# Grouped attention: spread and values issued ahead of the second pass of scores

## The reference

```python
q = rope((h @ Wq).reshape(B, S, 32, 128), pos)         # 32 query heads
k = rope((h @ Wk).reshape(B, S, 4, 128), pos)          # 4 key heads, 8 query heads each
v = (h @ Wv).reshape(B, S, 4, 128)
scores = einsum('bqhd,bkhd->bhqk', q, repeat(k)) / sqrt(128)   # causal mask
attn = softmax(scores, axis=-1)
o = einsum('bhqk,bkhd->bqhd', attn, repeat(v)).reshape(B, S, 32 * 128) @ Wo
x = resid + o
```

## Time and profile before

| | |
|---|---|
| time, median of 3 runs | 1534.93 us (1533.66 to 1537.94) |
| the profiled execution's own time | 1537.94 us |
| its span, first to last instruction | 1536.2 us |
| granted TensorE clock, mean of the span | 0.937 of full speed |
| busy in the whole span | PE 1342.8, DVE 961.9, ACT 792.4, POOL 617.7 us |
| the 64 steps of grouped attention | from about 750 to 1200 us |

### The profile page before, as it was taken

One profiled execution on the slowest core, in us unless ns is written; L12 is line 12 of the kernel. 1 busy time (PEld: TensorE's weight loads), 2 busy tenths in 40 slices (PEclk: granted clock), 3 DMA queues, 4 the chain that ended last, 5 costly groups with the idle time before them and its releaser, 6 DMA issues. The chain is left out here.

```text
span 1536.2 us, 23871 instructions
## 1 busy us (share of the span) xinstructions
PE 1342.8 (87%) x8621; PEld 987.4 (64%) x8621; DVE 961.9 (63%) x1625; ACT 792.4 (52%) x1590; POOL 617.7 (40%) x550
## 2 busy tenths in 40 slices
PE   5788678899799579886789999999999869999998
PEld 4564455644388434433557777776777658888887
DVE  4763754558755587873677777877787554333443
ACT  2455104345532246664567777777877544445442
POOL 5110001101054511211566666666676445555553
PEclk8999779989999678996899999999999979999999
DMA  2000400020000100002000000000000023233231
GB/s 70 1 1 2 121 3 0 4 101 0 1 1 1 38 1 2 2 2 81 7 14 15 15 25 19 15 22 22 15 22 8 8 87 121 96 119 110 105 119 51
DMA packets 29492, 55.58 MB, mean 36 GB/s; under 512 B 6506, under 2 KB 16170, under 8 KB 29204
## 3 DMA queue, kind: packets, MB, share of 16 engines
q1 hardware_dynamic: 29396, 54.30, 11.0%
HBM read 52.98 MB, written 1.21 MB: 35 GB/s over the span
## 5 line engine op out<-in xcount | busy, mean ns | idle before, releaser
L2606 DVE TENSOR_TENSOR e_act<-e_gated,ps 128x512 f32<-128x512 f32 x66 | 45.4, 688 | 158.1 <-POOL e_gated L2411 158.1
L1839 POOL TENSOR_TENSOR a_raw<-a_prod 128x512 f32<-128x512 f32 x72 | 98.3, 1366 | 51.7 <-DVE a_prod L2243 51.7
L1844 POOL TENSOR_TENSOR a_q_low<-a_raw,a_q_high 128x512 fp32r<-128x512 f32 x64 | 82.8, 1294 | 87.2 <-ACT a_q_high L2103 87.2
L2240 DVE TENSOR_TENSOR a_prod<-ps,a_rot 128x512 f32<-128x512 f32 x72 | 49.7, 691 | 93.9 <-PE ps L1888 93.7
L2411 POOL TENSOR_TENSOR e_gated<-e_gate,e_wb 128x512 f32<-128x512 f32 x66 | 85.2, 1292 | 49.8 <-ACT e_gate L2532 44.5
L1848 POOL TENSOR_TENSOR a_o_low<-a_o,a_o_high 128x512 fp32r<-128x512 f32 x64 | 82.9, 1295 | 41.7 <-ACT a_o_high L2154 39.7
L2111 ACT ACTIVATE a_shift<-ident,a_nmax 128x128 bf16<-128x128 f32 x256 | 81.9, 390 | 32.3 <-DVE a_nmax L2252 32.0
L2402 POOL TENSOR_TENSOR e_we_low<-e_we,e_we_high 128x768 fp32r<-128x768 f32 x33 | 60.8, 1842 | 89.5 <-ACT e_we_high L2537 85.5
L1606 DVE SCALAR_TENSOR_TENSOR m_acc<-ps,m_conv_w,m_acc 128x1020 f32<-128x1020 f32 (+2 forms) x60 | 76.0, 1275 | 31.3 <-ACT m_acc L1526 29.9
L1360 PE MATMUL ps<-m_ln_T,m_win 128*128 128x512 f32 x192 | 88.8, 618 | 4.2 <-DMA m_win<-in_m_winT 3.5
L601 DVE TENSOR_REDUCE x_nmax<-ps 128x2 bf16<-128x512 f32 x128 | 82.5, 689 | 11.2 <-PE ps L371 10.9
(11 more groups left out here) (431 smaller groups left out, 4271.2 us busy)
## 6 DMA issues: line engine op xcount, KB each, us to landing
e_wb<-token_weights SPq DMA_DIRECT2D x32, 512.0 KB, 3.9
e_we<-in_experts SPq DMA_DIRECT2D x33, 384.0 KB, 3.1
a_wq<-in_a_wq SPq DMA_DIRECT2D x16, 256.0 KB, 2.7
a_wo<-in_a_wo SPq DMA_DIRECT2D x16, 256.0 KB, 2.8
m_win<-in_m_winT SPq DMA_DIRECT2D x2, 1024.0 KB, 8.8
nf_pickU<-in_nf_pickU SPq DMA_DIRECT2D x2, 768.0 KB
nf_raw<-in_ffn_w SPq DMA_DIRECT2D x3, 352.0 KB
x<-in_x SPq DMA_DIRECT2D x4, 256.0 KB, 6.6
```

The lines of the kernel that those rows point to most:

```text
L1839: e.tensor_tensor(raw[:, i % 2, :], prod[:, i % 2, 0, :], prod[:, i % 2, 1, :], ALU.add).then_inc(s_raw, 1)
L1844: e.tensor_tensor(low_part, raw[:, i % 2, :], high_part.bitcast(F32), ALU.subtract).then_inc(s_xl, 1)
```

## The change

In TensorE's loop of the grouped attention, spread and values of step n - 4 are issued between the first scores of step n and the second scores of step n - 1, where they came behind both. Nothing else differs.

```diff
                 if n < N:
                     first_scores(n)
-                if 0 <= n - 1 < N:
-                    scores(n - 1)
                 if 0 <= n - PV < N:
                     spread(n - PV)
                     values(n - PV)
+                if 0 <= n - 1 < N:
+                    scores(n - 1)
                 for i in [*of_step.get(n, ())][:1]:
                     piece(i)
                 if 0 <= n - PO < N:
```

## The result

The changed kernel takes 1586.87 us (median of 4 runs, 1585.38 to 1593.71) against 1536.43 us before (4 runs): a ratio of 1.0341, 95% interval 1.0308 to 1.0374. The direction was forecast, the size was not: 1570.5 us with a range up to 1583. The two profiled executions stand 47.4 us apart (spans 1536.2 and 1583.6).

The account below looks back on a forecast made before the run. TensorE was taken to bound the stage, busy 392.14 of 405.00 us. Pairs behind keys 6.5, usual even steps 24.5, long splits 4.2 and step 4's 0.4 sum to 35.6 us; on 1534.93 that gives 1570.5 us, range 1560 to 1583.

Parts of the forecast that it names:

- The even steps: Usual pairs: values still wait for VectorE's division, then second scores follow; 1.36 us each in 18 steps, 24.5 us.
- Odd steps: Division ends 0.1 us before values could start, and ScalarE's exponentials keep 0.7 us of cover; cost 0.
- Pairs behind keys: Six pairs behind a piece of keys: 1.41 us less 0.33 from a 0.48 us split; 1.08 each, 6.5 us.
- The long splits: VectorE's split of inverses, 1.60 us instead of 0.48: 1.12 us per lost start; share kept, three steps, 4.2 us.
- the trace agrees: VectorE's split against GpSimd's sum: issue order decides who waits, and the edit leaves the order of these starts unchanged.
- The ends of the loop: First and last steps, where TensorE already waits for exponentials: 0.4 us for step 4, 0 from step 60 on.
- Steps 61 to 66 have gaps of their own: 0: Last steps of the loop: existing gaps were to absorb the moved scores, at no cost.
- The terms for step 4 and 60: Existing waits for exponentials absorb delay: step 4 costs 1.41 less 0.86, rounded down to 0.4 us; step 60 costs 0.
- (d): Rival: waits lower TensorE's granted clock, a tenth of the stage's columns at half clock, 39 us, 1610 us; 2%.
- (a): Rival: TensorE gets past the waiting spread and does the scores meanwhile; cost 0, 1535 us; 2%.
- (b): Rival: earlier values release division, low part and projection, closing TensorE's 12.86 us of gaps; at best 1522 us; 2%.
- (e): Rival: the chain is less tight than read, so half the price appears, 1553 us; 5%.

Follow-up runs that it names:

- spread_ahead: Kernel before with only spread moved ahead of the second scores, values left behind them; 1572.86 us, ratio 1.0267.
- values_ahead: Kernel before with only values moved ahead of the second scores, spread left behind them; 1589.31 us, ratio 1.0336.
- ordered_odd: Kernel before with the new order in odd steps only, and GpSimd waiting in even steps for VectorE's split; 1530.98 us, ratio 0.9967.
- odd_only: Kernel before with the new order in odd steps only, even steps in the old order; 1554.89 us, ratio 1.0137.
- ordered_new: Changed kernel, with GpSimd waiting in even steps for VectorE's split before its sum; 1577.98 us, ratio 1.0250 to the kernel before.
- filler_new: Changed kernel with 12 matmuls of a projection's form added in each of steps 4, 5 and 6; 1572.85 us, ratio 1.0289 to the kernel before.
- ordered_piece_old: Kernel before, old order, with the step's first piece right behind first scores and GpSimd waiting for the split; 1519.30 us, ratio 0.9900.
- ordered_old: Kernel before, old order, with GpSimd waiting in even steps for VectorE's split before its sum; 1523.70 us, ratio 0.9923.
- even_only: Kernel before with the new order in even steps only, odd steps in the old order; 1584.58 us, ratio 1.0339.

## Why the prediction was right in kind and wrong in size

- **The even steps.** Right, mechanism and size. Plain pairs grew by 1.43 us, 1.36 forecast; most of the difference is the second scores, which take 1.51 us behind values instead of 1.41 behind first scores. The 25 even steps from 10 to 58 were forecast at 32.75 us and came to 33.9 (396.89 - 362.99 between the sums of step 9 and 59). That three plain splits would be long again was luck: they are those of steps 14, 18 and 54, where they were 18, 32 and 46. spread_ahead and values_ahead have the pair lengths of the same chain to within 0.2 us, and with the piece early the price is gone from these steps.
- **Odd steps.** Right in plain pairs: the exponentials kept their place, and plain pairs of ordered_odd take 13.5 to 13.6. Behind a piece of keys the order in the odd step alone costs 0.66 us a pair (14.93 over 14.27), since TensorE waits 1.2 us for the division there.
- **Pairs behind keys.** 1.07 for 1.08 (15.30 to 16.37). The prediction's 0.48 us for these splits came true because the order of the two starts changed: before, GpSimd's sum starts 0.02 to 0.04 us ahead of the split, after, 0.04 to 0.05 behind it. That contradicts its own sentence that nothing in the edit changes that order. Against a kernel without long splits the price is 2.1 (14.27 to 16.37).
- **The long splits.** Step 4's is no toss: GpSimd starts within 0.02 us of it and it is long in both kernels. Of the tosses 3 of 22 were lost before, 4 of 28 after, 17 of 28 in odd_only, with the same 0.04 to 0.05 us between the starts; the unit price (1.1 us) was right, the odds are not steady. They do have a part in the profiled loss: step 60's split became a long one (1.1), and the low clock behind steps 4 and 60, 1.6 us each, is not in ordered_new, which has short splits there. That is up to 4.3 of the 46.0 us; that the long splits brought the low clock about is argued. The prediction's "the trace agrees" on the order of issue is too strong: at 878.06 VectorE starts first and its split is the one that lasts long.
- **The ends of the loop: the step that failed.** The prediction put "Steps 61 to 66 have gaps of their own: 0", step 60 at 0 and step 4 at 0.4, and priced step 6 as a plain one. Steps 4 to 6 cost 6.6 us for 1.8 (7.65 with the pair behind, for 2.84), step 60 and later 4.5 for 0. Of 46.0 us of loop that is 9.3 of the 10.4 that the sum of 35.6 lacks. The terms for step 4 and 60 would have held with short splits (0.48 and 0.32 in ordered_new); those for steps 5, 6, 62 and 64 would not. What stood there instead: the low clock three times, 1.6 us each by the blocks behind it (values and scores of step 4 last 4.26 us, 776.30 to 780.56, for 2.7 elsewhere), 4.8 together; steps 5 and 6 with waits 1.2 and 1.4 us longer than in plain steps (1.19 for none, 2.21 for 0.79), as no projection runs while VectorE rotates, which leaves 1.5 us over forecast and low clock; steps 62 and 64 with 1.4 us (0.6 and 0.8 in ordered_new too), where the split waits for ScalarE and the division ended 1.0 us ahead of values in the kernel before, less than the 1.41 us of scores that moved; a long split in step 60, 1.1. These make 8.8 of the 9.3.
- **The clock.** The rival (d) had 2% and was priced for the whole stage; what came was three short falls, 4.8 us. filler_new shows for steps 5 and 6 shorter waits and no fall, though its own 1.6 us can't be told from that of the waits there. What decides whether the clock falls stays open. The length of the wait in front of it alone does not: the waits for long splits at 862, 893 and 1179 us, 1.9 us each, and the 2.22 us at 801 left the granted clock at 1.00, the 1.90 at 1225 did not.
- **The other rivals.** (a) did not come: TensorE stood for the split in all 26 even steps with scores behind spread that needed nothing from it. In the Trainium skill ("TensorE: Matmul & The Clock Gate") the rule on the order of matmuls that the prediction cites stands under The mechanism, just ahead of the section that it names; these waits agree with it. (b), a gain, and (e), half the price, did not come either.
- **The rest** of the median, 50.4 us against 47.4 between the profiles, is scatter of executions: the kernel before ran from 1525.77 to 1543.87 us over all comparisons. Within a kernel the time mostly goes with the mean granted clock of the span, about 1 us for 0.001: the kernel before took 1525.77 us at 0.946 and 1538.00 at 0.935 in the last comparison, ordered_piece_old, with no long split in its trace, 1512.52 at 0.943 and 1523.96 at 0.933. That the number of long splits makes most of the scatter is not borne out: ordered_new, without any in its trace, ranges over 12.1 us.

## What to carry to other kernels

Before a block is moved ahead of another, look at what releases it: here an end 0.05 to 0.1 us ahead of its start, in all even steps up to 60, said that the block in front of it was the cover, and the whole block became the price. Price the first and the last turns of a pipelined loop one by one: a block that covers a wait in the middle (here the projection) may be missing there. And where the lengths of two engines' instructions depend on which of them gets going first, within a tenth of a microsecond, order them by a semaphore before anything is compared: an added wait made this kernel 0.8% faster.

## What was not expected of the hardware

- The split (two SBUF inputs, 128x256) takes 0.48 us and GpSimd's sum then 1.58, or 1.60 and 1.27. In both cases shown VectorE starts 0.05 us ahead. The Trainium skill ("SBUF — State Buffer", Who interferes with whom) says that issue order decides who blocks. The lengths agree nearly: the pair takes 1.63 or 1.60 us, the two alone 0.48 + 1.28 = 1.76. The starts agree in part. In all kernels without GpSimd's wait the split was long in 71 of 71 cases in which GpSimd started between 0.23 us ahead of it and 0.02 behind, and in 27 of 225 in which GpSimd started 0.04 to 0.05 us behind. So within 0.05 us the starts in the trace don't tell who blocks, and the outcome differed within one execution.
- With the wait (ordered_old) both engines take their own length, 0.48 and 1.28 us, one behind the other: 885.13 to 886.98, 1.85 us. Where VectorE won the toss the pair took 1.63 us (881.44 to 883.07). So GpSimd ends a little later with the wait than in a won toss, and no split in this trace is long.
- TensorE's granted clock fell to about half for 2 to 4 us behind waits of 2.85, 2.21 and 1.90 us, at a cost of 1.6 us each, and not behind other waits of 1.9 and one of 2.22 us. The 2.22 us wait was followed by 1.00 in the kernel before and by 0.57 in ordered_old, and even_only has both outcomes behind waits for the split of 2.00 us (1074 and 849 us).
